# Cross values' tile of full width, and a later place for the last norm's transpose and logits

## The reference

```python
def mha(xq, ctx, wq, wk, wv, wo, bo):        # 16 heads of 64, inner width 1024
    attn = softmax(q @ k.T / sqrt(64)); return concat_heads(attn @ v) @ wo + bo
def first(x, t, context):                    # adaln: layernorm with scale and shift from t
    h1 = adaln(x, t, norm1); x = mha(h1, h1, attn1) + x
    h2 = adaln(x, t, norm2); x = mha(h2, context, attn2) + x      # context: 77 rows a batch
    h3 = adaln(x, t, norm3); return glu_ff(h3) + x                # gelu(gate) * a @ w2
x = x + first(layernorm(x), cond, ctx)
# second: a mixture of 7 routed experts and a shared one; top 2 of softmax(layernorm(x) @ wr.T + rb)
x = x + moe_a(layernorm(x))
x = x + slots(cond, ctx, layernorm(x))       # three rounds of slot attention
x = x + moe_b(layernorm(x))                  # 8 experts, top 1
```

## Time and profile before

| | us |
|---|---|
| median of 3 runs (lowest, highest) | 979.17 (976.92, 979.4) |
| the profiled execution | 978.34 |
| its span | 976.5 |
| first phase, in the span | to about 574 |
| busy PE / DVE / ACT / POOL, share of the span | 82 / 58 / 54 / 37 % |

### The profile page before, as it was taken

How to read it: one execution, slowest core, us unless ns; L and a number is a source line. 1 busy time by engine, 2 the same in 40 slices (tenths; PEclk the granted TensorE clock), 3 DMA queues, 4 the chain that set the end, 5 groups by cost and what they waited for, 6 DMA issues and landing times.

```text
span 976.5 us, 18039 instructions
## 1 busy us (share of the span) xinstructions
PE 801.4 (82%) x5701; PEld 655.0 (67%) x5701; DVE 568.3 (58%) x1941; ACT 526.2 (54%) x1139; POOL 359.6 (37%) x559
## 2 busy tenths in 40 slices
PE   6978898999996999789796669899996877762594
PEld 5756686777874787578575545799855666652493
DVE  2557785677863667477466453333367877886112
ACT  3555565667663665466365332233527888861362
POOL 1223443334331323233265415266621322224463
PEclk9999898999997999899898769999965879795697
DMA  8514304340700420120221013488450000000474
GB/s 269 171 52 146 126 14 144 115 156 23 249 1 27 144 75 1 44 53 10 61 75 44 11 44 115 120 249 250 142 184 0 1 1 1 1 1 27 141 205 133
DMA packets 82055, 88.53 MB, mean 91 GB/s; under 512 B 6155, under 2 KB 69851, under 8 KB 81323
## 3 DMA queue, kind: packets, MB, share of 16 engines
q1 hardware_dynamic: 78475, 80.19, 27.3%
q0 software_dynamic: 3488, 7.20, 2.1%
HBM read 69.03 MB, written 35.17 MB: 107 GB/s over the span
## 4 chain that ended last, share of the span: by engine, by line
PE 47%; DVE 19%; ACT 10%; issue 8%; DMA 7%; POOL 6%; SPq 3%; DVEq 0%; POOLq 0%; ACTq 0%
DMA v_all<-sb_v_rows 5%; PE bank L964 5%; PE bank L707 4%; PE bank L674 4%; PE bank L680 3%; DVE sb_smax L1472 3%; DVE sb_row_sum L1481 3%; PE bank L697 3%; PE bank L747 3%; PE bank L972 2%; PE bank L1073 2%; PE bank L1081 2%; DVE sb_st_all L1779 2%; PE bank L925 2%; POOL sb_expd L1956 2%
## 5 line engine op out<-in xcount | busy, mean ns | idle before, releaser
L1956 POOL TENSOR_TENSOR sb_expd<-sb_expd,sb_rden 128x512 f32<-128x512 f32 (+1 forms) x128 | 112.0, 877 | 290.1 <-DVE sb_rden L1485 290.0
L1472 DVE TENSOR_REDUCE sb_smax<-bank 128x4 f32<-128x512 f32 (+1 forms) x128 | 74.1, 579 | 69.5 <-PE bank L707 47.3
L2048 POOL TENSOR_TENSOR sb_rstd_all<-sb_rsq_all,sb_halves 128x4 f32<-128x4 f32 x44 | 45.2, 1026 | 133.2 <-DVE sb_rsq_all L1786 133.2
L1195 ACT ACTIVATE sb_expd<-sb_shifted 128x512 f32<-128x512 f32 (+1 forms) x128 | 69.6, 544 | 30.2 <-DVE sb_shifted L1475 28.7
L1481 DVE TENSOR_REDUCE sb_row_sum<-sb_expd 128x4 f32<-128x512 f32 (+1 forms) x128 | 73.0, 570 | 8.0 <-ACT sb_expd L1195 8.0
L1475 DVE TENSOR_TENSOR sb_shifted<-bank,sb_smax 128x512 f32<-128x512 f32 (+1 forms) x128 | 75.0, 586 | 4.4
L674 PE MATMUL bank<-sb_h1T,sb_watt 128*128 128x128 f32 x512 | 71.2, 285 | 4.7 <-DMA sb_watt<-att_w 2.4
L674 PEld LDWEIGHTS bank<-sb_h1T,sb_watt 128*128 128x128 f32 x512 | 63.1, 195 | 9.6 <-DVE sb_xb L1461 3.7
L964 PE MATMUL bank<-sb_blk_xT,sb_up_w 128*128 128x128 f32 x456 | 57.1, 275 | 0.0
L2014 POOL DMA_INDIRECT back_a<-sb_blk_y,sb_dest_a x38 | 37.0, 973 | 48.8 <-issue 25.8
L964 PEld LDWEIGHTS bank<-sb_blk_xT,sb_up_w 128*128 128x128 f32 x456 | 54.0, 192 | 0.0
(11 more groups left out here) (260 smaller groups left out, 2006.7 us busy)
## 6 DMA issues: line engine op xcount, KB each, us to landing
sb_up_w<-gate_up SPq DMA_DIRECT2D x38, 384.0 KB
sb_v<-v_all SPq DMA_DIRECT2D x16, 576.0 KB, 5.6
rows_b<-pad_b SPq DMA_DIRECT2D x7, 1105.0 KB, 10.1
rows_a<-pad_a SPq DMA_DIRECT2D x7, 975.0 KB, 8.4
sb_up_w<-w1b SPq DMA_DIRECT2D x23, 256.0 KB
v_all<-sb_v_rows SPq DMA_DIRECT2D x14, 308.0 KB
sb_blk_x<-rows_a SPq DMA_DIRECT2D x38, 65.0 KB, 3.3
sb_picked<-back_a SPq DMA_DIRECT2D x4, 512.0 KB, 5.5
```

The costliest lines, as they stand in the source:

```text
L1195: act.activation(exp_of(i, s, j), shifted[:, u % 2, :, 0:n], ACT.Exp, scale=DH ** -0.5).then_inc(exp_done, 1)
L1472: dve.tensor_reduce(smax[:, u % 2, :], s_in, X, ALU.max).then_inc(max_done, 1)
L1956: pool.tensor_tensor(e, e, rden[:, u % 2, :].unsqueeze(2).broadcast_to([P, QH, n]), ALU.mult).then_inc(norm_done, 1)
L2048: pool.tensor_tensor(rstd_all[:, c], rsq_all[:, 0, c], halves[:, c], ALU.pow).then_inc(root_ready[k], 1)
```

## The change

The tile for the cross values becomes full width (128 x 2048). It takes the place of `down` in `moe_w`, and the tile of 128 x 1024 goes. So `v2_2` has no wait of its own; `v2_0` still waits for the stores of all earlier blocks. The loads of `gate_up` and `down` move from the program's start to iteration 15, in SP's queue behind the read of batch 15's values and a wait for all stores. `tri` stays at the start with a semaphore of its own.

The transpose `zT` and the product `logit` of a batch move from step 11 of its last iteration to steps 2 and 3 of the next one, DVE's addition of the bias from step 10 to step 4. The loop gets one more iteration (18) for the last batch's. `h2T` moves from step 0 to step 1, behind `g2_5`. `v1_0` moves from step 10 to step 8, ahead of `ffout`, and `v1_1` from step 11 to step 10. The `rank` products and with them POOL's early writes come one iteration later.

```diff
 FILL = [
-    (("h2T",), ("g2_5",)),
-    (("a2_0", "a2_1"), ("a2_2", "wo2", "rank")),
-    (("q1_1", "b2_0"), ("k1_0",)),
-    (("k1_1", "a2_3"), ("q1_0", "b2_1")),
+    ((), ("g2_5",)),
+    (("h2T", "a2_0", "a2_1"), ("a2_2", "wo2", "rank")),
+    (("q1_1", "b2_0", "zT"), ("k1_0",)),
+    (("k1_1", "a2_3"), ("q1_0", "b2_1", "logit")),
...
-    (("wo1",), ("g2_2", "ffout")),
+    (("wo1",), ("g2_2", "v1_0", "ffout")),
     (("v2_2",), ("hT",)),
-    ((), ("v1_0", "v2_3")),
-    (("zT", "v1_1"), ("logit",)),
+    ((), ("v2_3", "v1_1")),
+    ((), ()),
 ]
...
-AT = {"wo2": 2, "gate": 5, "gelu": 6, "glu": 6, "sums": 9, "logit": 10, "exp": 5, "rank": 2}
+AT = {"wo2": 2, "gate": 5, "gelu": 6, "glu": 6, "sums": 9, "logit": 4, "exp": 5, "rank": 2}
...
-RANK_AT = [last + 3 for _, last in PARTS["a"][:-1]]
+RANK_AT = [last + 4 for _, last in PARTS["a"][:-1]]
...
-    for i in range(-1, B + 2):
+    for i in range(-1, B + 3):
...
+        v2_rows = moe_w[:, 2 * CA * P:2 * CA * P + 2 * INNER]
-        v2_rows = sb1("v2_rows", P, INNER)
...
-            sp.dma_start(gate_up[:, :], A["gate_up"][EA]).then_inc(ld_moe, 16)
-            sp.dma_start(down[:, :, :, :], A["down"]).then_inc(ld_moe, 16)
-            sp.dma_start(tri[:, :], A["tri"]).then_inc(ld_moe, 16)
+            sp.dma_start(tri[:, :], A["tri"]).then_inc(ld_tri, 16)
...
                 values(i)
                 if 1 <= i <= PAD_PARTS:
                     empty_rows(i - 1)
+                if i == max(V2_BLOCK) + 1:
+
+                    sp.wait_ge(v2_stored, 16 * v2_stores(len(V2_BLOCK)))
+                    sp.dma_start(gate_up[:, :], A["gate_up"][EA]).then_inc(ld_moe, 16)
+                    sp.dma_start(down[:, :, :, :], A["down"]).then_inc(ld_moe, 16)
...
                     if name == "v2_0":
                         from_one(act, v2_stored, 16 * v2_stores(n))
-                    if name == "v2_2":
-                        act.wait_ge(v2_stored, 16 * (v2_stores(n) + len(v2_pieces(n))))
-                    empty(i, name, v2_rows[0:last, half % 2 * 512:(half % 2 + 1) * 512], lambda t: t[0:last, :])
+                    empty(i, name, v2_rows[0:last, half * 512:(half + 1) * 512], lambda t: t[0:last, :])
```

More of the change, by code:

```diff
@@ L72 @@
 UNIT_CHUNKS = [range(HEAD_END[j - 1] if j else 0, HEAD_END[j]) for j in range(QH)]
-AT = {"wo2": 2, "gate": 5, "gelu": 6, "glu": 6, "sums": 9, "logit": 10, "exp": 5, "rank": 2}
+AT = {"wo2": 2, "gate": 5, "gelu": 6, "glu": 6, "sums": 9, "logit": 4, "exp": 5, "rank": 2}
 STREAM = {n: s for s, names in (("A", "wo1"), ("B", "a2_0 a2_1 a2_2 a2_3 b2_0 b2_1 b2_2 b2_3 g2_0 g2_1 g2_2 g2_3 g2_4 g2_5 h2T v2_0 v2_1 v2_2 v2_3"),
-                                ("C", "wo2 h3T gate lin ffout zT logit"),
+                                ("C", "wo2 h3T gate lin ffout"), ("D", "zT logit"),
                                 ("X", "hT rank"), ("N", "q1_0 q1_1 k1_0 k1_1 v1_0 v1_1")) for n in names.split()}
@@ L156, in streams @@
 def streams(i):
-    return {s for s, b in (("A", i), ("B", i - 1), ("C", i - 2), ("N", i + 1)) if 0 <= b < B}
+    return {s for s, b in (("A", i), ("B", i - 1), ("C", i - 2), ("D", i - 3), ("N", i + 1)) if 0 <= b < B}
 def present(i, name):
@@ L423, in program @@
             sem(n) for n in ("ld_x", "ld_small", "ld_att1", "ld_att2", "ld_ff", "ld_ctx"))
-        ld_vo2 = sem("ld_vo2")
+        ld_vo2, ld_tri = sem("ld_vo2"), sem("ld_tri")
         ld_x_first, ld_rows, rows_added = sem("ld_x_first"), sem("ld_rows"), sem("rows_added")
@@ L499, in first_phase_over @@
         def first_phase_over(eng):
-            eng.wait_ge(emptied["dve"], PLAN[B + 1, "logit"][2])
+            eng.wait_ge(emptied["dve"], PLAN[B + 2, "logit"][2])
             eng.wait_ge(z_kept, B + 1)
@@ L551, in store_values @@
                         sp.dma_start(by_batch[b, k0:k1, 8 * half:8 * half + 8, :],
-                                     v2_rows[p0:p1, :].rearrange("p (h d) -> p h d", h=8)).then_inc(v2_stored, 16)
+                                     v2_rows[p0:p1, half * INNER:(half + 1) * INNER].rearrange("p (h d) -> p h d", h=8)).then_inc(v2_stored, 16)
             def load_values(b):
@@ L834, in fill @@
                 if name == "zT":
-                    pe.wait_ge(z_ready["C"], i - 1)
+                    pe.wait_ge(z_ready["C"], i - 2)
                     turn(i, name, zC)
@@ L846, in rank_sums @@
                 pe.wait_ge(hot_ready[x], part + 1)
-                pe.wait_ge(ld_moe, 48)
+                pe.wait_ge(ld_tri, 16)
                 first, last = PARTS[x][part]
@@ L888, in _ @@
             iteration(0, streams(0))
-            for i in range(1, B + 2):
+            for i in range(1, B + 3):
                 iteration(i, streams(i))
@@ L895, in flat @@
                 return t[:, 4 * g:4 * g + 4, :].rearrange("p b c -> p (b c)")
-            pe.wait_ge(ld_moe, 48)
+            pe.wait_ge(ld_moe, 32)
             def sh_turn(g):
@@ L1700, in iteration @@
                             softmax_sums(i, *summed(k))
-                    if k == AT["logit"] and "C" in S:
+                    if k == AT["logit"] and "D" in S:
                         filled(i, "logit")
-                        dve.tensor_tensor(tile(logits, c)[:, 0:EA], bank_of(i, "logit")[:, 0:EA], R["rb"],
+                        dve.tensor_tensor(tile(logits, i - 3)[:, 0:EA], bank_of(i, "logit")[:, 0:EA], R["rb"],
                                           ALU.add).then_inc(emptied["dve"], 1)
```

## The result

The changed kernel takes 939.61 us in the median of 4 runs (938.22 to 943.04), the one before 978.85 beside it; the ratio is 0.9608, interval 0.9577 to 0.9639. The forecast was 935.6 in a range of 923 to 953. The profiled execution took 940.69, its span is 938.9.

A forecast was written before the change was run, and what follows sets the result against it. No engine fills the span; ACT's waits for the store of cross values, with PE idle and then at half clock, were taken as the main loss. 978.34 - 37.0 - 6.5 = 934.8, 935.6 us against the median; range 923 to 953.

The forecast's parts named there:

- The five stalls, 37.0: Store waits gone in iterations 0, 3, 8, 11 and 13: gains of 5.5, 4.9, 10.1, 8.1 and 8.4 us.
- The bank wait of 1.0 for xb: At k1_0, which now needs the bank that DVE empties with xb: 1.0 us of new PE idle time.
- The split, 37.0 for the stalls and 6.5 for the rest: Whole kernel: 37.0 us gained from five store stalls, 6.5 from everything else by iteration, most of it the order.
- less 0.3 for the store wait still in it: Even value iterations: 30.49 us less 0.3 for a short store wait, taken as their price without a stall.
- From 12 to 13, a loss of 1.3: The rank product moved into iteration 13 makes zT wait for xb and k1_0 for the ranks' copy: 1.3 us lost.
- the rival of the clock: New short idle stretches lower PE's clock: 22.7 us more per plain iteration hit, three give 1003 us; chance 0.03.
- From 2 to 3, a loss of 0.15: Period from iteration 2 to 3, apart from the five stalls: 0.15 us lost.
- The end of the phase, 15 to 17, a gain of 2.4: Gains of 1.0 us from 15 to 16 and 1.4 from 16 to 17, zT and logit no longer ahead of wo2.
- Slack of the stores, 5 us: Iteration 9's v2_0: back-to-back stores end at 320.3 us at worst, it comes about 325, leaving 5 us.
- The rival of the moved stall: v2_0 or wo2 waits for back-to-back stores in two to four blocks, 3 to 6 us each: 948 to 960; chance 0.11.
- the signs of being wrong: New DMA wait at v2_0 or wo2, odd plain periods of 28 us and more, or mid-phase clock under 1.00.
- the new order gives nothing: Only the stalls' 37 us are gained, or less by bank waits up to 1 per iteration: 941 to 952; chance 0.18.

The follow-up runs named there:

- the second run: The changed kernel measured again, with no edit, on one chip beside the wide tile with the old order: 940.01 us, ratio 0.9590 to the kernel before.

## Why the prediction was right, and where it wasn't

The time was in the range and the sign and size were right. Up to the last gelu the profiled executions differ by 35.95 us (563.42 - 527.47) where 43.5 was forecast; another 1.65 came behind it, where nothing was forecast. By its steps, with what the trace of the changed kernel has in place of each:

- *The five stalls, 37.0.* To the gelu of iteration 2 (which holds the stall of iteration 0) 3.7 against 5.5; then 5.1, 10.1, 8.0 and 8.2 against 4.9, 10.1, 8.1 and 8.4. Sum 35.2. What is short is the start: its first 42 us are 1.3 later already, in products of the first weights. This stretch varies from run to run: the first scores start between 20.55 and 23.05 us in the traces, whatever the order and the tile.
- *Plain odd iterations, 1.1 each.* 1.2 and 1.26. The row maximum starts right behind zA, as worked out. From 10 to 11 it is 0.35 against 0.15.
- *The bank wait of 1.0 for xb.* PE's waits are 0.86 to 0.96 in the trace, and 0.8 to 1.0 an iteration when it was taken away. Its mechanism and size were right.
- *The split, 37.0 for the stalls and 6.5 for the rest.* This failed. The forecast for the changed kernel's value iterations (30.3, which by its own terms, 30.49 - 0.3, is 30.2, and 29.55; measured 30.35 and 29.60) was right, but the tile alone would have given 29.7 and 29.0. The step "less 0.3 for the store wait still in it" priced the short store waits at almost nothing (0.3 from 6 to 7); in the old order they were worth 0.8 there, 1.7 from 9 to 10 and 1.7 from 4 to 5, while in the new order they cost nothing. And the order's effect in value iterations was set at a small gain by the terms of the plain ones, where it is a loss of 0.6: no zC wait stands there to be removed, and the xb wait is added. Two errors of opposite sign in the same iterations, which one total can't show; that they cancelled was luck.
- *From 12 to 13, a loss of 1.3.* It was 4.2. The two bank waits were named; that together they would bring the clock down, was not. The argument against the rival of the clock, that it fell only behind idle time of 7.58, misread the rows: wo2 runs for 4.61 in the earlier trace rows behind waits of PE of 1.05, 1.08 and 0.46.
- *From 2 to 3, a loss of 0.15.* It was 1.4. ffout, which has the bank of wo1 now, waits 4.44 for xa; in the kernel before it didn't wait, and PE waited 2.06 and 1.81 behind it. Against the tile alone the v1 edits by themselves cost 1.1 here and the zT edits 0.8.
- *The end of the phase, 15 to 17, a gain of 2.4.* It was 0.25, at a clock of 0.71 against 0.83 from 15 to 16; what lowered it was not tested. But the one trace of the kernel before (37.6 for the two periods) is quick here: the old order takes 39.2 to 39.3 in the tile alone, twice, and with the stores cut, and the changed one 37.35 and 35.9. Against those the order gives 1.8 to 3.3, around the 2.4 forecast.
- *Moved loads, early writes, iteration 18: nothing.* No engine waits for the loads. The part behind the last gelu took 411.4 against 413.1, but 416.9 in the second run, so by time no less than some 5 us can be told from nothing there.
- *Slack of the stores, 5 us.* 5.8 (308.15 to 313.94). The rival of the moved stall had no case.
- *The signs.* The store wait, the logits' wait, iterations 8, 11 and 13 and the plain odd ones are as said. Of the signs of being wrong one came true in one place, the clock of 0.95 from 12 to 13, and the plain even iteration there takes 32.59, not 28.2.

Of the rivals, "the new order gives nothing" was given 0.18, with 941 to 952 us, and is what holds for the order within a few us; it came with a time that the tile's larger gain made up for.

## What to carry over

When a change has two parts that work on the same stall, price each alone as well as both together: a right total doesn't show that the reasons were right. In a ring of few buffers, the place of a product in the order is also a choice of whose buffer it waits for; write down for each use which use stands one ring earlier and which engine empties it, before moving anything. For a slow store look at the share of the DMA engines that is busy under it: cutting 53 rows into 48 and 5 took 8 us off one wait without moving a byte less. Short waits cost more than their length when they bring the clock down, so read the clock beside them.

## What the runs showed of the hardware

While a store of 53 rows runs, the DMA share reads 0.07 to 0.08 at 21 to 23 GB/s, in both kernels, which is about one engine of sixteen. As long as nobody waits for it, it costs PE nothing: PE's clock stayed at 1.00 and PE was busy for 6.00 of 6.00 us beside it.

The granted clock fell also without one long idle stretch. In the changed kernel's iteration 13, waits of 0.82, 1.50 and 0.51 us within 6.5 us were followed by a mean of 0.59 over 3 us. In the run with v1 moved only, waits of 0.43, 1.64 and 0.46 were followed by 0.74 over 6.5 us, and with the stores cut waits of 1.22 and 0.86 by scores of 2.08 instead of 1.16. Plain iterations with a single wait of about 1 us kept 1.00, and so did the tile alone from 10 to 11 with 0.36 and 0.96, and the run with zT behind the keys from 12 to 13 with 0.82 and 1.07.
